# Waiting for every fourth row transfer, a linear-attention loop two batches ahead, and paired last loads

## What is computed

```python
x = x + 0.5 * L0_ffn(layernorm(x))   # 8 experts, top 2, softmax gates, tanh gelu
x = x + L0_attn(layernorm(x))        # 16 heads of 8, rope, softmax
x = x + 0.5 * L0_ffn(layernorm(x))
x = x + 0.5 * L1_ffn(layernorm(x))   # 16 experts, top 2, capacity 640, erf gelu
x = x + L1_attn(layernorm(x))        # linear attention: elu+1 features, running over each batch row
x = x + 0.5 * L1_ffn(layernorm(x))
```

## Time and profile before

| | |
|---|---|
| median of 3 runs | 1687.96 us |
| lowest, highest | 1668.94, 1697.09 us |
| the profiled execution: its time | 1688.85 us |
| the profiled execution: its span | 1687.0 us |
| PE, DVE, ACT, POOL busy, share of the span | 73, 51, 44, 44% |
| granted TensorE clock, mean | 0.872 of full |

### The profile page before, as it was taken

One profiled execution on the slowest core, in us unless ns is written; L12 is line 12 of the kernel. 1 busy time (PEld: TensorE's weight loads), 2 busy tenths in 40 slices (PEclk: granted clock), 3 DMA queues, 4 the chain that ended last, 5 costly groups with the idle time before them and its releaser, 6 DMA issues.

```text
span 1687.0 us, 22666 instructions
## 1 busy us (share of the span) xinstructions
PE 1223.7 (73%) x7326; PEld 797.3 (47%) x7326; DVE 863.9 (51%) x2597; ACT 735.8 (44%) x1494; POOL 737.4 (44%) x988
## 2 busy tenths in 40 slices
PE   2208997389999999998199973239994666659991
PEld 2107887122223233223189862228783555538781
DVE  5442332698999999884223327722211566521213
ACT  3313443057677767776144433313331455423332
POOL 3683444021334545334534444644543155535452
PEclk9999999589999999999599995569997566669996
DMA  9725775443344435410357752323432012024326
GB/s 193 113 91 173 230 211 159 134 129 111 82 131 140 115 88 145 131 50 15 112 166 222 217 160 77 125 61 120 143 104 61 25 54 94 29 63 137 128 96 166
DMA packets 164836, 202.56 MB, mean 120 GB/s; under 512 B 19376, under 2 KB 132400, under 8 KB 164720
## 3 DMA queue, kind: packets, MB, share of 16 engines
q1 hardware_dynamic: 141040, 160.32, 34.3%
q0 software_dynamic: 18304, 37.65, 7.0%
q10 hardware_dynamic: 5376, 3.15, 0.7%
HBM read 133.88 MB, written 66.91 MB: 119 GB/s over the span
## 4 chain that ended last, share of the span: by engine, by line
PE 49%; DVE 17%; issue 16%; DMA 8%; SPq 3%; ACT 3%; POOL 3%; ACTq 1%; another core or an unknown queue 0%; POOLq 0%; DVEq 0%
PE PS L1190 15%; PE PS L1201 14%; DVE arena L1871 6%; DMA arena<-dispatched 4%; PE PS L1273 4%; PE PS L1248 4%; PE PS L1177 2%; DMA YC<-expert_out 2%; PE PS L1258 1%; PE PS L1236 1%; POOL expert_out L633 1%; DVE BST L1542 1%; DMA qk_products<-arena 1%; ACT arena L932 1%; POOL dispatched L792 1%
## 5 line engine op out<-in xcount | busy, mean ns | idle before, releaser
L633 POOL DMA_INDIRECT expert_out<-arena x316 | 302.4, 957 | 371.8 <-DVE arena L1779 273.8
L874 ACT ACTIVATE arena<-PS,arena 128x256 f32<-128x256 f32 (+1 forms) x440 | 238.8, 566 | 419.2 <-PE PS L1190 403.8
L932 ACT ACTIVATE arena<-PS 128x512 f32<-128x512 f32 x512 | 286.1, 595 | 129.7 <-PE PS L1248 125.3
L1871 DVE TENSOR_REDUCE arena<-PS 128x2 f32<-128x1024 f32 x256 | 302.2, 1218 | 12.3 <-PE PS L1260 10.3
L1201 PE MATMUL PS<-arena 128*128 128x128 f32 x2528 | 300.3, 274 | 3.6 <-DVE arena L1779 3.6
L1201 PEld LDWEIGHTS PS<-arena 128*128 128x128 f32 x2528 | 296.7, 191 | 8.3 <-issue 4.2
L1190 PE MATMUL PS<-arena 128*128 128x256 f32 (+2 forms) x1136 | 300.5, 412 | 0.0
L1779 DVE TENSOR_TENSOR arena<-PS,arena 128x256 f32<-128x256 f32 (+1 forms) x110 | 59.5, 541 | 422.8 <-PE PS L1201 415.3
L1190 PEld LDWEIGHTS PS<-arena 128*128 128x128 f32 x1136 | 197.9, 194 | 76.8 <-issue 63.2
L1248 PE MATMUL PS<-arena 96*128 96x512 bf16 x512 | 169.4, 386 | 8.6 <-ACT arena L932 4.9
L620 POOL DMA_INDIRECT dispatched<-arena x128 | 124.2, 970 | 101.1 <-DVE arena L1652 57.9
(11 more groups left out here) (273 smaller groups left out, 1454.6 us busy)
## 6 DMA issues: line engine op xcount, KB each, us to landing
arena<-experts SPq DMA_DIRECT2D x110, 578.0 KB
qk_products<-arena SPq DMA_DIRECT2D x48, 384.0 KB
arena<-qk_products SPq DMA_DIRECT2D x64, 288.0 KB
YC<-expert_out SPq DMA_DIRECT2D x48, 256.0 KB
arena<-dispatched SPq DMA_DIRECT2D x32, 322.5 KB
arena<-dispatched SPq DMA_DIRECT2D x78, 129.0 KB
arena<-qk_products SPq DMA_DIRECT2D x64, 128.0 KB
dispatched<-ZERO SPq DMA_DIRECT2D x16, 322.5 KB
```

The costliest lines, as they stand in the source:

```text
L633: pool.indirect_dma_start(YK, bass.IndirectOffsetOnAxis(ap=ID[:, r, s:s + 1], axis=0), YS[:, r, s, :], None).then_inc(s_yo[r], 16)
L874: act.activation(HT[:, c % PAIR, q, 0:S * P], hidden_chunk(S, q), func, bias=WE[:, r, 2 * DFF + q:2 * DFF + q + 1]).then_inc(s_g, 1)
L932: act.activation(PT[:, G % 2, j, k, :], bank(4 + k % 2), ACT.Exp, scale=float(1.0 / np.sqrt(HD))).then_inc(s_exp, 1)
L1871: dve.tensor_reduce(MX[:, G % 2, head:4:2, a], PS[:, 1024 * w:1024 * w + 1024].rearrange("p (a b) -> p a b", a=2), AX_X, ALU.max).then_inc ...
```

## The change

Three edits that don't meet each other.

1. In the loop of the first and third dispatch (L617), GpSimd waits ahead of transfers 4, 8, ... 60 until all transfers so far have landed.
2. The linear attention's loop begins at -2. ScalarE's and VectorE's preparation (gather, moments, centre, scale) and GpSimd's deviation are of batch i+2. TensorE turns batch i+1 at the start of the step, projects its queries behind `logits`, and its keys and values between `turn_out` and `project`. ScalarE copies the turned batch at the start, and its `features(i+1)` stand behind `out_rows(i)`. Two waits that guard bank 0 move by one batch.
3. The last loads are 8 transfers of 512 KB in place of 16 of 256 KB, with one semaphore for two groups.

Two semaphores that nothing used are gone as well.

```diff
@@ SyncE, the end
-            for b in range(NG):
-                cols = slice(b * GT, b * GT + GT)
-                sp.dma_start(YF[:, 0, cols], src[:, 0, cols, :]).then_inc(s_yl[b], 16)
+            for c in range(NG // 2):
+                cols = slice(c * 2 * GT, (c + 1) * 2 * GT)
+                sp.dma_start(YF[:, 0, cols], src[:, 0, cols, :]).then_inc(s_yl[c], 16)
@@ GpSimd, moe
                     for k in range(2):
+                        n = 2 * t + k
+                        if n % 4 == 0 and n > 0:
+                            pool.wait_ge(s_disp, 16 * (2 * NT * (f > 0) + n))
                         pool.indirect_dma_start(buf, bass.IndirectOffsetOnAxis(ap=SLOT[:, k, t:t + 1], axis=0),
                                                 XR[:, k, t, :], None).then_inc(s_disp, 16)
@@ GpSimd, linear
-                for i in range(-1, NG + 2):
+                for i in range(-2, NG + 2):
                     if batch(i - 2):
                         dispatch(i - 2, 0)
-                    if batch(i + 1):
-                        deviation_of(i + 1, s_l1v, s_l1d)
+                    if batch(i + 2):
+                        deviation_of(i + 2, s_l1v, s_l1d)
@@ ScalarE, linear
-                for i in range(-1, NG + 1):
+                for i in range(-2, NG + 1):
+                    if batch(i + 1):
+                        front_rows(i + 1)
                     if batch(i - 1):
                         batch_centre(i - 1)
                         batch_scale(i - 1)
                         batch_rows(i - 1)
                         second_rows(i - 1)
-                    if batch(i + 1):
-                        front_centre(i + 1)
                     if batch(i):
                         out_rows(i)
                     if batch(i + 1):
-                        front_scale(i + 1)
-                        front_rows(i + 1)
                         features(i + 1)
+                    if batch(i + 2):
+                        front_centre(i + 2)
+                        front_scale(i + 2)
@@ ScalarE, second_experts: four loads of two groups each, then
-                    act.wait_ge(s_yl[b], 32)
+                    act.wait_ge(s_yl[b // 2], 32)
@@ TensorE, linear
-                    if b >= 2:
-                        pe.wait_ge(s_l2c, b - 1)
+                    if b >= 3:
+                        pe.wait_ge(s_l2c, b - 2)
...
-                    pe.wait_ge(s_l1c, min(r + 2, NG))
+                    pe.wait_ge(s_l1c, min(r + 3, NG))
...
                 for i in range(-1, NG + 1):
+                    if batch(i + 1):
+                        turn_front(i + 1)
                     if batch(i):
                         sums(i)
...
                     if batch(i - 1):
                         logits(i - 1)
+                    if batch(i + 1):
+                        queries(i + 1)
                     if batch(i):
                         turn_out(i)
+                    if batch(i + 1):
+                        keys_values(i + 1)
+                    if batch(i):
                         project(i)
-                    if batch(i + 1):
-                        turn_front(i + 1)
                     if batch(i - 1):
                         ranks(i - 1)
-                    if batch(i + 1):
-                        queries(i + 1)
-                        keys_values(i + 1)
@@ VectorE, linear
-                for i in range(-1, NG + 1):
+                for i in range(-2, NG + 1):
                     if batch(i):
                         features(i)
-                    if batch(i + 1):
-                        gather(i + 1, 0)
+                    if batch(i + 2):
+                        gather(i + 2, 0)
                     if batch(i):
                         by_head(i)
-                    if batch(i + 1):
-                        gather(i + 1, 1)
-                        moments(i + 1, s_l1v)
+                    if batch(i + 2):
+                        gather(i + 2, 1)
+                        moments(i + 2, s_l1v)
```

More of the change, by code:

```diff
@@ L276, in build @@
         s_dve, s_pool_chain = sem("dve_step"), sem("pool_step")
-        s_var, s_sd = sem("variance_ready"), sem("deviation_ready")
         s_xs, s_tr, s_xt = sem("xs_ready"), sem("xs_transposed"), sem("xt_ready")
@@ L296, in build @@
         s_out = sem("out_stored")
-        s_yl, s_ys = [sem(f"last_y_loaded{b}") for b in range(NG)], sem("last_y_scaled")
+        s_yl, s_ys = [sem(f"last_y_loaded{c}") for c in range(NG // 2)], sem("last_y_scaled")
         s_proj, s_rope, s_rot = sem("projected"), sem("rope_read"), sem("qk_roped")
@@ L1079, in second_experts @@
                     act.wait_ge(s_yo[r], scattered0(f + 1, r))
+                for c in range(NG // 2):
+                    cols = slice(c * 2 * GT, (c + 1) * 2 * GT)
+                    act.dma_start(YF[:, 1, cols], src[:, 1, cols, :]).then_inc(s_yl[c], 16)
                 for b in range(NG):
-                    cols = slice(b * GT, b * GT + GT)
-                    act.dma_start(YF[:, 1, cols], src[:, 1, cols, :]).then_inc(s_yl[b], 16)
-                for b in range(NG):
-                    act.wait_ge(s_yl[b], 32)
+                    act.wait_ge(s_yl[b // 2], 32)
                     for t in range(b * GT, b * GT + GT):
@@ L1548, in combine_last @@
                 for b in range(NG):
-                    dve.wait_ge(s_yl[b], 32)
+                    dve.wait_ge(s_yl[b // 2], 32)
                     for t in range(b * GT, b * GT + GT):
```

## The result

The changed kernel takes **1721.95 us** (median of 4 runs, 1713.81 to 1725.70) against 1692.53 before (4 runs, 1668.94 to 1697.26). The ratio is 1.0253, with a 95% interval of 1.0135 to 1.037: it is slower, and whether by 2% or more the interval leaves open. Ratios and intervals here take only the runs within 1.5% of the fastest of their kernel, while medians and ranges take all, so a ratio can differ from that of the medians. The forecast was 1688.6 with a range from 1668 to 1708, so the time lies outside it. The profiled execution took 1720.61 us with a span of 1718.8; before it was 1688.85 and 1687.0 us.

What follows compares the result with a forecast made beforehand. TensorE (73% busy) was taken to pace expert tiles and attention, with other waits in the third dispatch, linear attention and end. Terms +16 - 14 - 1.4 = +0.6 moved the median 1687.96 to 1688.6, range 1668 to 1708.

Steps and rivals of the forecast that it cites:

- The price of a wait: Dispatch loop, both dispatches: each landing wait costs 1.7 us more than now, about 2.0 idle; bounds 1.14 to 2.5.
- the walk: Step-by-step timing: GpSimd's first-dispatch groups of 13.65 us, last landing at 126.6; for the linear loop, a step of 18.6.
- its slower rival: Both dispatches: landing under load makes every wait dearer; 1725 us at d=3; chance 0.10 for d 2.1-2.9, 0.04 above.
- The prediction's estimate from the Trainium skill: First dispatch: HBM access at high load adds 1.8 us per wait, some 11 us for six waits; not in the sum.
- The cover by SyncE: First dispatch: row loads stand behind SyncE's expert weights, so issuing them as late as 128.1 costs nothing.
- The forecast 0 for the first dispatch: First dispatch: the waits cost 0, as the last landing at 126.6 is inside 128.1; 10 at wait cost 2.5.
- The fills over the first tiles: First expert layer: GpSimd's two delayed fills hold small VectorE operations of the first tile; +1, bounds 0 to 4.
- The linear loop: Linear attention: a step falls from 20.4 to 18.6 us; -14 in all, bounds 0 to -26.
- The end: Last loads: ScalarE issues four transfers instead of eight; -1.4, the middle of -2.8 and 0.
- the two readings: Last loads: the queue holds ScalarE by number of transfers (-2.8) or by bytes (0).

Runs made afterwards that it cites:

- The paced fill: Kernel before with waits in the first dispatch only, SyncE also waiting for each of the 16 large zero fills to land: 1690.7 us (one profile).
- late fills and waits: Kernel before with waits in the first dispatch only and the 16 large zero fills moved into the attention: 1696.51 us, ratio 1.0124.
- late fills and no waits: Kernel before with only the large zero fills moved into the attention: 1673.87 us, ratio 0.9956.
- filler: Unread matmuls in TensorE's linear-loop gaps: 1666.05 us in the kernel before, 1658.1 in the changed kernel without its waits.

## Why the prediction was wrong

**The price of a wait: right where nothing stands ahead, wrong by 10 us beneath the fill.** The step that failed is "I take 1.7, as the scatter is the same instruction with the same kind of target", used for both dispatches. Sum the fifteen idle times: 33.8 us in the third dispatch, 65.6 in the first; the prediction's 2.0 each makes 30. In the third dispatch that is 3.8 too little, and 15 + 3.8 = 18.8 meets the measured 18.1. In the first, 35.6 too little: 29.7 in the three waits beneath the fills, 6.8 in the two beside tails and weights. Put into the walk, the last landing moves from 126.6 to 162.2; it was at 161.0. The walk was right, the landing in it was not. The prediction had the fact at hand, and listed it for its slower rival: the fills keep the transfers' engines full. It set against it that a row transfer is only 66 KB. The paced fill shows why that does not help: the landing of a small transfer is late by the fills that stand outstanding. The prediction's estimate from the Trainium skill, 1.8 us more for each of six waits beneath the fill, had the direction and not the size: three waits paid 9 to 10.6 us more each. The rival's form, one price d for all waits with its turn at 2.9, was wrong too. Its 1725 (+32 in the third dispatch, +18 in the first) came near the time by two errors that cancel: the third paid 18, the first layer 38.

**The cover by SyncE: right in the kernel before, gone in the kernel after.** "They can be issued up to 124.08 + 7.05 - 3.03 = 128.1 with the same landing" took SyncE's issue of the weights at 121.73 as a fixed time. It moved to 91.50, because the routing itself ran faster with GpSimd's transfers broken up by waits. VectorE's slots of the first groups (timeline) stand at 16.95 and 30.65 before, 16.91 and 27.25 after, and then 9.1 apart instead of some 12.3. It's not the fills: with late fills and waits they are 9.1 apart as well, with late fills and no waits 12.2 on the mean. In the third dispatch they are 10.5 apart with waits and 11.8 without. And without waits VectorE is busy for 31.7 (late fill) and 30.4 (before) of the 60 us from 15 to 75, against 38.9 with late fills and waits. Among what grows are VectorE's waits for its own last instruction. The same operation, for the third and for the fourth group of the kernel before:

```profile
33.89 0.19 DVE L1623 TENSOR_TENSOR arena<-arena 128x32 f32<-128x32 f32 x1
...
47.58 0.19 DVE L1623 TENSOR_TENSOR arena<-arena 128x32 f32<-128x32 f32 x1 [1.49 <-DVE arena L1622]
```

Back-to-back issue on GpSimd, which the waits break up, slows the others down; how, no run shows. So the cover was made by the very thing that the change removes. What gained from the faster routing was only work that waits for the rows later. One credit is left: the rows land 2.2 us after their issue instead of 7.05, so of 37.1 us late issue TensorE saw 32.3. At the forecast price this credit would have been enough: with late fills and waits TensorE's first matmul on rows is at 130.59, where before it was 131.27. The forecast 0 for the first dispatch fell by the price, not by the cover.

**The fills over the first tiles: right place, and about the right size.** I put +1 with bounds to 4. VectorE stood for 5.8 us, but the scatters behind it came only 1 to 2 us late. That leaves some 4 of the 38.2 - 32.3 = 5.9 us unexplained. From the first matmul to the last scatter the layer took 157.7 to 163.1 us in the profiles without waits there, 159.1 before, and 165.0 in the changed kernel, so much of it may be scatter.

**The linear loop: right sign, wrong reason for the size.** The forecast step of 18.6 came out as (1479.24 - 1357.90) / 7 = 17.3, with three of the eight queries at the full clock, which the walk did not know. What failed is the premise that the old step is 20.41. It is 20.4 or 17.1. With the old loop at full clock its stage is 183.1, and the new one, whose clock alternates, has 180.3 to 184.6: nearly nothing. Against the profile before, at half clock, it is 22. In medians it is 21. The new loop alternates in all five of its profiles without filler and never stays at half clock. Of the old loop most runs seem to be at half, by their mean granted clock: in the runs of before that list one, those near 1663 have 0.884 to 0.887, those from 1690 on 0.866 to 0.874. The range of 1669 to 1697 in the runs before would fit this too; those runs list no clock. I had read that spread as the measurement's own.

**The end: -1.6 alone, -1.9 in the whole, near the -1.4.** Which of the two readings was right? The middle between them was right by luck. The queue holds ScalarE more by bytes than by number: four double loads take it 6.69, and eight single ones took 8.60, of which the first four were out after 2.1.

```profile
1694.83 6.69 ACTq L1085 DMA_DIRECT2D arena<-expert_out  x4
1701.11 1.14 DVE L1556 SCALAR_TENSOR_TENSOR X<-arena,GATE,X 128x128 f32<-128x128 f32 x4 [14.77 <-DMA arena<-expert_out]
1701.56 2.45 ACT L1089 ACTIVATE arena<-arena,GATE 128x128 f32<-128x128 f32 x8 [25.75 <-DMA arena<-expert_out]
```

VectorE's first data come 8.6 after the last scatter instead of 6.8, and ScalarE follows 0.45 later instead of 4.2.

**Sum.** Predicted +16 - 14 - 1.4; measured +56.3 - 22.0 - 1.9, with -0.6 elsewhere: +31.8. The terms of edit 1 and of edit 2 were both missed, and the range, made from one price for all waits, was too narrow on its upper side.

## What to carry to other kernels

- The price of waiting for a transfer is set by what stands outstanding when it is issued, here another engine's fills. Before you add a wait, list what the other queues have in flight there; a bulk fill nobody waits for becomes part of every wait.
- Cover read from the old trace holds only if the change leaves alone what makes it. Ask whether the covering work is itself late because of what you remove.
- A loop with idle TensorE has a duration for each clock. Look at one repeated matmul over several steps, and at the spread of the runs with their clocks, before you take a step's length from one profile. Cheap filler in the gaps was worth as much here as a new order.

## What the hardware showed that I had not expected

- A row transfer of 66 KB is reported 2.3 us after its issue with nothing ahead, 11.7 behind a queue of 322.5 KB fills from another engine that go out one in 2.8 us. With at most one of them outstanding GpSimd idles 2.0 to 5.2 us for it, where it idled 11 to 12.6.
- GpSimd's transfers in close order slow the routing on other engines: groups of 9.1 us with pauses, some 12.3 without, with VectorE's single instructions no longer (0.19 us both times) but waits of up to 1.5 us between them. By which way, no run here tells.
- Two GpSimd fills of 6.92 us held a VectorE operation on 128x2 values for 5.83 us. Cut into 32 pieces of about 0.5 us, they held it for 0.28.
- The old linear loop runs at 20.4 or 17.1 us a step for the same instructions. In six of its eight profiles without filler it keeps one of the two from the second batch on, in two it changes on the way.
